# VectorE's order signals in two attentions with 16 short heads: drains left out, each maximum waits for its own unit's bias signal

## The reference, cut to what matters

```
# layer 0: windows of 64 queries, which see their own and the previous window's 64 keys
scores = einsum('bhnqd,bhnkd->bhnqk', qb, k2) * scale
scores = where(valid, scores + bias, -inf)
p = softmax(scores, axis=-1)
out = einsum('bhnqk,bhnkd->bhnqd', p, v2)

# layer 1: all 256 keys, with a bias by relative position
scores = einsum('bhqd,bhkd->bhqk', Q, K) / sqrt(D_K) + rel_bias[...]
out = einsum('bhqk,bhkd->bhqd', softmax(scores, axis=-1), V) @ Wo.T + bo
```

## Time and profile before

| | us |
|---|---|
| median of 3 runs | 1752.79 |
| lowest and highest of them | 1752.48, 1757.74 |
| the profiled execution | 1758.61 |
| its span, first to last instruction | 1756.5 |

### The profile page before, as it was taken

One profiled execution on the slowest core, in us unless ns is written; L12 is line 12 of the kernel. 1 busy time (PEld: TensorE's weight loads), 2 busy tenths in 40 slices (PEclk: granted clock), 3 DMA queues, 4 the chain that ended last, 5 costly groups with the idle time before them and its releaser, 6 DMA issues. The chain is left out here.

```text
span 1756.5 us, 44283 instructions
## 1 busy us (share of the span) xinstructions
PE 1542.0 (88%) x16972; PEld 1183.8 (67%) x16988; DVE 1327.8 (76%) x2187; ACT 1218.3 (69%) x2065; POOL 1099.6 (63%) x661
## 2 busy tenths in 40 slices
PE   6899996999999599999999569899999999999985
PEld 5577774666666366666666347777777777777774
DVE  4899984554555499999998488788888888888753
ACT  2577774444444478888888258888888888888863
POOL 1666762444444388888888367666777667777614
PEclk7899998999999789999999589999999999999997
DMA  5000000000000410000000001111111111111113
GB/s 170 2 3 3 3 3 15 8 15 7 7 7 1 151 30 2 14 2 14 2 13 11 12 16 29 25 26 26 26 26 26 26 26 26 26 26 26 26 26 102
DMA packets 56839, 44.14 MB, mean 25 GB/s; under 512 B 28152, under 2 KB 47900, under 8 KB 56388
## 3 DMA queue, kind: packets, MB, share of 16 engines
q1 hardware_dynamic: 56644, 41.45, 8.9%
HBM read 17.75 MB, written 4.23 MB: 13 GB/s over the span
## 5 line engine op out<-in xcount | busy, mean ns | idle before, releaser
L832 POOL TENSOR_TENSOR a_prob<-a_prob,a_top 128x1024 f32<-128x1024 f32 x128 | 239.8, 1895 | 58.5 <-DVE a_top L1023 58.4
L1235 POOL TENSOR_TENSOR e_hh<-e_h,e_hh 128x512 fp32r<-128x512 f32 x112 | 144.2, 1290 | 166.8 <-ACT e_hh L1219 165.4
L1494 POOL TENSOR_TENSOR i_qk<-i_qk,i_rt 128x1024 f32<-128x1024 f32 x64 | 152.1, 2376 | 46.5 <-DVE i_rt L1937 41.9
L1504 POOL TENSOR_TENSOR i_qk<-i_qk,i_rn 128x1024 f32<-128x1024 f32 x64 | 122.6, 1916 | 83.8 <-DVE i_rn L1916 83.8
L1256 DVE TENSOR_TENSOR e_h<-ps,e_sg 128x512 f32<-128x512 f32 x112 | 77.3, 690 | 123.9 <-PE ps L1118 104.3
L1793 ACT ACTIVATE i_prob<-i_prob,i_top 128x128 f32<-128x128 f32 x512 | 156.4, 391 | 16.1 <-DVE i_top L1925 14.2
L1202 ACT ACTIVATE e_sg<-ps 128x512 f32<-128x512 f32 x112 | 67.0, 598 | 141.4 <-PE ps L1118 141.4
L978 ACT ACTIVATE a_probT<-ps 128x1024 f32<-128x1024 f32 x128 | 131.1, 1024 | 45.3 <-PE ps L908 45.3
L1020 DVE TENSOR_TENSOR a_prob<-ps,a_table 128x1024 f32<-128x1024 f32 x128 | 148.6, 1203 | 13.7 <-PE ps L900 13.5
L1491 POOL TENSOR_TENSOR i_qk<-i_raw,i_rot 128x1024 f32<-128x1024 f32 x59 | 140.1, 2375 | 25.0 <-issue 25.0
L908 PEld LDWEIGHTS ps<-ident,a_prob 128*128 128x128 f32 x1024 | 113.4, 142 | 62.7 <-ACT a_probT L978 48.8
(11 more groups left out here) (305 smaller groups left out, 4390.5 us busy)
## 6 DMA issues: line engine op xcount, KB each, us to landing
i_V<-i_V SPq DMA_DIRECT2D x96, 130.0 KB, 2.3
a_table<-skew_scratch SPq DMA_DIRECT2D x2, 2048.0 KB, 12.6
X<-in_L_attn_x SPq DMA_DIRECT2D x4, 512.0 KB, 6.1
a_table<-in_c_l_table SPq DMA_DIRECT2D x1, 2048.0 KB, 8.3
e_xs<-Y SPq DMA_DIRECT2D x8, 256.0 KB, 2.3
i_ms<-Y SPq DMA_DIRECT2D x16, 128.0 KB, 2.4
i_ms<-Y SPq DMA_DIRECT2D x16, 112.0 KB, 2.4
out_dram<-X SPq DMA_DIRECT2D x7, 256.0 KB, 2.3
```

Source lines behind the costliest of these rows:

```text
L832: nc.gpsimd.tensor_tensor(s, s, top[:, slot].unsqueeze(2).broadcast_to([P, HG, KW]), ALU.subtract).then_inc(shifted, 1)
L1235: nc.gpsimd.tensor_tensor(hh[0:n, b % HBUF, 1, :], h[0:n, b % HBUF, :], hh[0:n, b % HBUF, 0, :].bitcast(F32), ALU.subtract).then_inc(h_lo, 1)
L1494: nc.gpsimd.tensor_tensor(s, s, rt[:], ALU.add).then_inc(rotated, 1)
L1504: nc.gpsimd.tensor_tensor(flat, flat, rn[:, T // TPB % 2, T % TPB].unsqueeze(2).broadcast_to([P, 2 * FH, FD]), ALU.mult).then_inc(qk_done, 1)
```

## The change

Three drains go: in both attentions the one on every step between adds and maxima, and in `window_attention` also the one behind the product of `normalise`. The drain between reciprocal and product stays, as do those inside `between`. In both attentions `row_max(n)` gets a wait for `biased >= n + 1`, a count that VectorE itself raises when `add_bias(n)` is done. That is two added waits for a pair of units, against one drain taken out on the even step and one (bias attention) or two (window attention) on the odd one. No compute instruction, DMA or buffer is added, removed or moved.

```diff
@@ window_attention, vector
             def row_max(n, slot):
+                dve.wait_ge(biased, n + 1)
                 nc.vector.tensor_reduce(top[:, slot], prob[:, slot], AX.X, ALU.max).then_inc(max_done, 1)
 
             def normalise(T):
@@
                 dve.drain()
                 nc.vector.tensor_tensor(oT[:, T % 4, :], ps[:, 6, 0:P], rden[:, :], ALU.mult).then_inc(o_sb, 1)
-                dve.drain()
@@
                     add_bias(n, n % NBUF)
                     add_bias(n + 1, (n + 1) % NBUF)
-                dve.drain()
                 if step % 2 == 0 and 0 <= n < UNITS:
                     row_max(n, n % NBUF)
                     row_max(n + 1, (n + 1) % NBUF)
```

## The result

| | before | after |
|---|---|---|
| median of 6 runs, us | 1751.53 | 1738.9 |
| lowest and highest | 1747.51, 1757.74 | 1735.9, 1744.9 |
| profiled execution, span | 1758.61, 1756.5 | 1735.9, 1733.8 |

The ratio is 0.9934, 95% interval 0.9906 to 0.9961: faster by 11.6 us (6.8 to 16.5). I had said 5.4 us, and a range that ended at 1742.0. The direction was right, the size was not.

What follows compares the result with a forecast made beforehand. TensorE was taken to set the window attention's pace, a loop over GpSimd without VectorE the bias attention's. Savings of 4.1 and 1.2 us, taken as 5.4 with small idle gaps, gave 1747.4 us, range 1742 to 1754.

Steps and rivals of the forecast that it cites:

- the rival of no gain: Whole kernel: the pause stays without the drain, or TensorE's pace swallows the savings; time 1752.8 us, chance 0.28.
- the bias attention's middle: 15 batches in the middle of the bias attention, adds 22.09 us apart, where VectorE's saving was to bring nothing.
- the loop that was shortened: Bias attention: mask, two subtractions, scale, projection and scores, without VectorE, were said to set the period of 22.09 us.
- the first of the sum: Window attention: TensorE's 3.25 us wait for VectorE was to shrink by one pair's saving, 0.46 us.
- The clock step: Window attention: TensorE's slow spell behind the 3.25 us wait goes too, 1.8 us more, time 1745.6 us; chance 0.12.
- The other waits of rows 4: Window attention: TensorE's five further waits for VectorE, predicted to give 0.5, 1.07, 1.07, 0.57 and 0.42 us.
- small idle gaps: Small idle gaps that were to go as well, raising the predicted saving from 5.3 to 5.4 us.
- the predicted 0.3: Start of the bias attention: two drains fewer ahead of the adds that TensorE's scores wait for, 0.3 us.
- 0.9 through: End of the bias attention: of about 1.3 us saved by VectorE, TensorE's transposes were to let 0.9 us through.
- the 1752.8 that I started from: The whole kernel's time in us if the change brought nothing, from which the 5.4 us were taken.

Runs made afterwards that it cites:

- `bias_half`: The change made in the bias attention alone, against the kernel before, window attention as before; ratio 0.9995 (0.9976 to 1.0014).
- `product_drain_out`: The kernel before with only the drain behind the product of `normalise` in the window attention taken out; ratio 0.9987 (0.9972 to 1.0003).
- the edit of GpSimd's program: Bias attention's scale one subtraction earlier; ratios to the kernel before: 0.9834 (1720.4 us) made in the kernel after, 0.9961 made in the kernel before.

## Why the prediction was wrong

- The prices of the drains were right: 0.17 us from adds to maxima, 0.3 from product to add, 0.19 to the reciprocal where I had 0.24 and 0.17. That the wait for VectorE's own signal costs 0 was right. The pause went with the drain, so the rival of no gain is out.
- That the bias attention's middle gives nothing was right; it is now shown, by the loop that was shortened. VectorE waits before one pair of adds in four there, not before nearly every one.
- The step that failed is the first of the sum, "one pair's saving counts: 0.46". It took the length of L272 as fixed. The wait fell by 2.03 us: 0.46 to 0.5 from the pair, and 1.54 from the freed add (1.97 - 0.43). The row was in VectorE's timeline, 1.97 us beside neighbours of 0.42 with the same shape, and GpSimd's start 0.21 us ahead of it was in the timeline of all engines. I read neither as a thing that could change.
- The clock step I had as a rival of 0.12, because 2.8 us was nearer to 3.25 than to 1.23. With the freed add the wait is 1.22, and the step was gone: 1.58 us more. I had priced it at 1.8, half of the 3.6 us behind the wait, but in that profile the first sums still ran partly at full clock (0.52 us, against 0.66 in `bias_half`). This place gave 3.61 us in all where I had 0.46. That is 3.15 of the window attention's miss of 3.8 (7.9 against 4.1).
- The other waits of rows 4: I had 3.6 us, and they gave 4.27. The waits themselves fell by 0.70, 1.07, 1.07, 0.57 and 0.42, 3.83 in all; the rest comes from the four unmarked ones of 0.17 one tile later, less some 0.1 that TensorE still pauses at three of the places. "Between them TensorE runs without a pause" was thus not quite so; what I added for small idle gaps, 0.1, was too little.
- The bias attention gave 2.2 us, not 1.2, and 2.46 between the two profiles shown. At its start TensorE's third scores come 6.98 us behind the first add instead of 7.29, the predicted 0.3, and its fourth 13.09 instead of 14.18, another 0.8, because its clock rises one instruction earlier. That can come without the change too: in `product_drain_out` the fourth come at 13.28. From the last waiting add to the last small sum it is 32.91 against 34.25, 1.3 us where I had let 0.9 through; that repeats (34.0 to 34.3 in five kernels, 32.9 in four).
- The range ended 3 us too high at the bottom. It had the clock step in it, not a hold that ends. The 10.1 us of the stretches, taken off the 1752.8 that I started from, give 1742.7, at the edge of the range; the rest of the way to 1738.9 is within the spread of runs. The rival of the clock step came true, but not in the way I gave for it: no wait of 2.8 us ever came about.

## What to carry to other kernels

Drains in a loop cost VectorE 0.17 to 0.25 us each here, and only where another engine waits for VectorE does that reach the end; the loop that sets the period has to be found by starts that touch ends. Before taking a duration as fixed, compare it with the same shape elsewhere in the trace: one that is four times as long may be held by another engine, and a shift of 0.2 us may free it, or catch another. A saving that a stage swallows may come out later, when what bounds it is shortened: here the edit of GpSimd's program took 0.4% off the kernel before and 1.1% off the kernel after.

## What the runs showed of the hardware that I had not expected

- A VectorE add of 128x256 with two SBUF inputs took 0.43 us when it started ahead of GpSimd's 1.9 us multiplication and 1.97 (or 1.48, started half a microsecond later) when it started behind. It ended 0.28 us after GpSimd's each time. GpSimd's next instruction then took 2.08 us instead of 1.90.
- In the window attention TensorE came back at clock 0.5, or fell to it within its first sums, in all the profiles where it had been idle for 3.19 to 5.17 us, and stayed at 1.00 where it had been idle for 1.22 or 1.45. Between these, elsewhere, both happen (1.86 us: down; 3.02 us: not).
- A second drain directly behind another cost 0.05 us, the first 0.25.
- Of one kernel, executions spread over 15 us (1739.8 to 1755.3 in 35 runs of the kernel before). How much of that lies in the first 45 us, where the profiles of different kernels differ by up to 7 us, the run times don't tell.
